# A two-layer attention and expert kernel with its engine loops written out, its waits on constants and its extra semaphore steps left out

## The chip, the cores and the metric

The kernel runs on one core of a Trainium2 chip, in one launch. The metric is the device time of that launch in microseconds, the median of several runs. The five engines of the core run streams of their own (TensorE or PE, VectorE or DVE, ScalarE or ACT, GpSimd or POOL, SyncE or SP), and meet only at semaphores. ScalarE, GpSimd and SyncE also issue DMA transfers from their streams.

## The reference

The input x is 16 batches of 512 tokens with 128 features in float32. Each of two layers adds an attention and an expert network to x, both taken of the same normalised rows:

```python
x = L0_attn_x
xn = _layernorm(x, axis=-1)
x = x + _L0_attn_ref(xn, ...) + _L0_ffn_ref(xn, ...)
xn = _layernorm(x, axis=-1)
x = x + _L1_attn_ref(xn, ...) + _L1_ffn_ref(xn, ...)
```

Layer 0 attention is causal, with 4 query and 2 key heads of 32 features, normalised queries and keys. Its expert network takes the 2 best of 16 experts of 256 hidden features (GELU). Layer 1 attention has 16 query and 4 key heads of 8 features, without a mask, a position factor on queries and keys, and the softmax's shift by the row maximum. Its expert network takes the best of 8 experts of 352 hidden features (SiLU, gated).

## The kernel before

The program is a row of blocks, and between blocks all engines meet: setup, layer 0 attention, a group table, the layer 0 experts, layer 1 attention, a second group table, the layer 1 experts.

**Attention, both layers.** The 16 batches are a software pipeline of which every engine writes its part as `body(i, o)` for batch 2i + o: the batch's own scores, exponentials and values, the end of the batch before (output projection and store), and the start of the next one to three (load, statistics, norms, projection, transposes). The helper `bodies` runs it: batches 0 to 2 and 13 to 15 are straight code, batches 3 to 12 are a hardware loop of five passes with two batches each, so each engine jumps back four times.

```python
def bodies(eng, body):
    for o in range(3):
        body(0, o)
    with eng.Fori(1, 6) as i:
        body(i, 1)
        body(i, 2)
    for o in range(13, NB):
        body(0, o)
```

In layer 0 a batch goes round a ring: VectorE's `square_sums` (L372) frees GpSimd's `factors` (L529 to L534); on GpSimd follow the scatter of the rows of the batch before to the experts' buffers (L544) and `norms` of the batch after (L512 to L518); VectorE normalises its rows (L357), PE transposes and projects them, ScalarE squares the projections, and VectorE sums them again. In layer 1 each batch has 64 score tiles on PE twice, once for the row maximum (L1834, reduced by VectorE at L1605, eight steps ahead) and once for the exponentials (L1806, ScalarE at L1511), and 16 steps of values (L1819). VectorE's stream also holds the router (`choose`, L1657, its first instructions once a batch, at step 0) and the statistics of the batch after next (L1696, step 2), which wait for GpSimd's `combine` (L1354 to L1358) of rows gathered by indirect DMA (L1343).

**Experts, both layers.** Tokens are packed in groups of 256 rows of one expert, 80 groups in layer 0 and 40 in layer 1, in a ring of 8 buffers. `pipeline` writes 8 groups as one turn of the ring: the first and the last turn are straight code, the eight (layer 0) or three (layer 1) between are a loop with `i` in a register. SyncE loads the rows of a group from an address in a table, ScalarE stores the results of the group before (L1087) and then issues the weights for the group eight ahead, also from the table (L1081, L1082), between its own activations (L1078). PE transposes the rows (L1035, copied by VectorE at L1112), multiplies by the first weights (L1047) and by the second (L1057).

**Waits.** With `i` in a register, a wait such as `wait_ge(x_used, b + 1)` needs its number computed in registers first. Where such a wait stands ahead of a DMA, an indirect DMA or another wait, the kernel puts a step of its own between them, an instruction that only counts up a semaphore that nobody reads. `passed` is that step, and `link_apart` is `link` (count up, wait for it on the same engine) with that step behind it:

```python
def passed(eng, count):
    eng.sem_inc(count, 1)
```

These steps are carried out in straight code as well, since the bodies are the same functions.

Of the kernel before, what the change touches and what calls it, by code (L numbers as in the profile page):

```python
# [10 lines left out]
ALU = mybir.AluOpType  # L11
# [5 lines left out]
NB, L = 16, 512  # L17
# [7 lines left out]
QKV0 = D + 2 * KV0 * DH0  # L25
# [15 lines left out]
NBUF = 8  # L41


class Chain:
# [25 lines left out]
def passed(eng, count):  # L70


    eng.sem_inc(count, 1)  # L73
# [143 lines left out]
def layer0_attention(nc, k, x_d, base_d, meta_d, xs_d):  # L217


    with ExitStack() as ctx:  # L220
# [72 lines left out]
        with nc.Block() as block:  # L293

            @block.sync
            def _(sp):
                def load(i, o):
                    b, h, p = batch(i, o)
                    sp.wait_ge(x_used, b + 1)
                    passed(sp, k.passed_sp)  # L300
                    sp.dma_start(x[:, p], x_d[bass.ds(b * L, L), :].rearrange("(t p) d -> p t d", p=P)).then_inc(x_in[p], 16)

                def store_meta(i, o):
                    b, h, p = batch(i, o)
                    sp.wait_ge(meta_ready, b + 1)
                    passed(sp, k.passed_sp)
                    sp.dma_start(meta_d[bass.ds(b * P, P), :], meta[:, p]).then_inc(meta_out[p], 16)

                def store_base(i, o):
                    b, h, p = batch(i, o)  # L310
                    sp.wait_ge(wo_used, b + 3)
                    passed(sp, k.passed_sp)
# [21 lines left out]
            def _(dve):  # L334
# [4 lines left out]
                def statistics(i, o):  # L339
# [6 lines left out]
                    ln.link_apart(last)  # L346
# [43 lines left out]
                def choose(i, o):  # L390

                    b, h, p = batch(i, o)
                    heads.link_apart(nc.vector.tensor_tensor(lg[:], prj[:, :, QKV0:PRJ0],
# [3 lines left out]
                    heads.link_apart(last)  # L397
# [100 lines left out]
            def _(pool):  # L498
# [3 lines left out]
                def norms(i, o):  # L502
# [8 lines left out]
                    passed(pool, k.passed_pool)  # L511
# [3 lines left out]
                    ln.link_apart(nc.gpsimd.tensor_tensor(tmp4[:, 2], tmp4[:, 1], mv[:, :, 1], ALU.mult))  # L515
# [5 lines left out]
                def factors(i, o):  # L521
# [7 lines left out]
                    fc.link_apart(nc.gpsimd.tensor_tensor(ftmp[:, 0], ss[:], bc, ALU.mult))  # L529
# [8 lines left out]
                def scatter(i, o, c):  # L538
                    b, h, p = batch(i, o)
                    if c == 0:  # L540
                        pool.wait_ge(meta_ready, b + 1)
                        passed(pool, k.passed_pool)
# [363 lines left out]
def expert_ffn(nc, k, layer, xs_d, ys_d, w_d, name, meta_d=None, base_d=None):  # L906
# [12 lines left out]
    with ExitStack() as ctx:  # L919
# [21 lines left out]
        with nc.Block() as block:  # L941

            @block.sync
            def _(sp):
# [13 lines left out]
                with sp.Fori(1, n_grp // NBUF) as i:  # L958
# [10 lines left out]
            def pipeline(eng, rows_of, up, down):  # L969
# [17 lines left out]
                with eng.Fori(1, last) as i:  # L987
# [9 lines left out]
            def _(pool):  # L997
                def put_rows(j, i, q):

                    pool.wait_ge(y_sb, j + 1)  # L1000
                    passed(pool, k.passed_pool)
# [157 lines left out]
def layer1_attention(nc, k, ys_d, base_d, meta_d, rf_d, rows2_d, qparts_d, kparts_d):  # L1159
# [6 lines left out]
    with ExitStack() as ctx:  # L1166
# [67 lines left out]
        with nc.Block() as block:  # L1234

            @block.sync
            def _(sp):
                def load(i, o):
                    b, h, p = batch(i, o)
                    if not (isinstance(b, int) and b < 2):  # L1240
                        sp.wait_ge(comb_done, b - 1)
                        passed(sp, k.passed_sp)
# [3 lines left out]
                def put_k(i, o):  # L1246
                    b, h, p = batch(i, o)
                    sp.wait_ge(kl_ready, b + 1)
                    passed(sp, k.passed_sp)
                    sp.dma_start(kparts_d[p].rearrange("j r l -> r j l"), kp[:]).then_inc(k_out[p], 16)  # L1250

                def put_q(i, o):
                    b, h, p = batch(i, o)
                    sp.wait_ge(ql_ready, b + 1)
                    passed(sp, k.passed_sp)
                    sp.dma_start(qparts_d[p].rearrange("j r l -> r j l"), qp[:]).then_inc(q_out[p], 16)

                def k_stack(i, o):

                    b, h, p = batch(i, o)  # L1260
                    if not (isinstance(b, int) and b < 2):
                        sp.wait_ge(s_ps, 64 * (b - 1))
                        passed(sp, k.passed_sp)
                        sp.wait_ge(mx_ps, 64 * (b - 1))
                        passed(sp, k.passed_sp)
                    sp.wait_ge(k_out[p], 16 * (h + 1))
                    passed(sp, k.passed_sp)
# [4 lines left out]
                def q_stack(i, o):  # L1272
# [3 lines left out]
                    passed(sp, k.passed_sp)  # L1276
# [16 lines left out]
                def shift(i, o, g):  # L1293
                    b, h, p = batch(i, o)
                    sp.wait_ge(sh_ready, 4 * b + g + 1)
                    passed(sp, k.passed_sp)
# [35 lines left out]
            def _(pool):  # L1332
                def gather(i, o, rows, s=None):
# [7 lines left out]
                    passed(pool, k.passed_pool)  # L1341
# [18 lines left out]
                def norms(ln, i, o):  # L1360
# [5 lines left out]
                    passed(pool, k.passed_pool)  # L1366
# [3 lines left out]
                    ln.link_apart(nc.gpsimd.tensor_tensor(tmp4[:, 2], tmp4[:, 1], mv[:, :, 1], ALU.mult))  # L1370
# [16 lines left out]
                def v_rows(i, o):  # L1387
# [4 lines left out]
                    passed(pool, k.passed_pool)  # L1392
# [3 lines left out]
                def k_parts(pc, i, o):  # L1396
# [4 lines left out]
                    pc.link_apart(nc.gpsimd.tensor_tensor(kr[:], k32[:], kp[:, 0, :], ALU.subtract))  # L1401
# [3 lines left out]
                def q_parts(pc, i, o):  # L1405
                    b, h, p = batch(i, o)
                    pool.wait_ge(qT_sb, b + 1)
                    pc.link_apart(nc.gpsimd.tensor_tensor(qr[:], q32[:], qp[:, 0, :], ALU.subtract))
# [4 lines left out]
                def normal_rows(i, o):  # L1413
# [5 lines left out]
                    passed(pool, k.passed_pool)  # L1419
# [5 lines left out]
                def keep_xn(i, o):  # L1425
# [4 lines left out]
                    passed(pool, k.passed_pool)  # L1430
                    nc.gpsimd.tensor_copy(row[:, p, :, 0:D], xn[:, p]).then_inc(kept_xn, 1)

                def scatter(i, o, t, s=None):
# [6 lines left out]
                    passed(pool, k.passed_pool)  # L1440
# [156 lines left out]
            def _(dve):  # L1597
# [52 lines left out]
                def choose(i, o):  # L1650
# [3 lines left out]
                    passed(dve, k.passed_dve)  # L1654
# [3 lines left out]
                    pro.link_apart(last)  # L1658
# [31 lines left out]
                def statistics(i, o):  # L1690
# [6 lines left out]
                    ln.link_apart(last)  # L1697
# [374 lines left out]
```

## Time and profile before

| | us |
|---|---|
| median of 3 runs | 1857.05 |
| lowest, highest run | 1851.42, 1863.5 |
| profiled execution | 1872.54 |
| its span, first to last instruction | 1870.8 |
| mean granted TensorE clock | 0.933 of full |
| PE, VectorE, ScalarE, GpSimd busy | 1590.7, 1231.6, 939.0, 831.1 |
| DMA transfers | 165.01 MB |

A program was profiled once, and all rows below are of that execution. Busy time is what each engine's instructions took; register, branch and semaphore instructions do not count as busy and are seen only as idle time of the engine ahead of its next instruction. That idle time is given in brackets behind a row with what ended it; "issue" means that no semaphore's update explains it. Line numbers are those of the kernel before. Layer 0 attention lies from about 70 to 485 us, its experts from 505 to 680 us, layer 1 attention from 685 to 1655 us, its experts from 1685 to 1860 us.

### The profile page before, as it was taken

How to read it: one execution, taken by the hardware profiler on the slowest of the kernel's cores; microseconds unless marked ns; L12 is line 12 of the kernel's file. 1: busy time of each engine (PE TensorE's matmuls, PEld its weight loads, DVE VectorE, ACT ScalarE, POOL GpSimd, SP SyncE). 2: the span in 40 equal slices, each digit the busy share in tenths (PEclk: the TensorE clock that was granted, in tenths of full speed). 3: DMA queues.
4: the chain of work that ended last, by engine and by line, in shares of the span. 5: the costliest groups of instructions: out<-in, count | busy, mean ns of one | idle time of the engine just before them, and what ended most of it. 6: DMA issues, size and time to landing. Idle time of an engine off the chain costs nothing. (4 is left out here: it accounts for less than half of the span.)

```text
span 1870.8 us, 35103 instructions
## 1 busy us (share of the span) xinstructions
PE 1590.7 (85%) x9488; PEld 825.8 (44%) x9488; DVE 1231.6 (66%) x3176; ACT 939.0 (50%) x1790; POOL 831.1 (44%) x987
## 2 busy tenths in 40 slices
PE   1688888888499954899999999999999999928997
PEld 0344444444298852233333333333333333308996
DVE  4466566657333335688888797888878899714443
ACT  1233433434143321577777676776767777712221
POOL 2465566556140024555555555455545541003444
PEclk9999999999799985699999899999999999969998
DMA  2011111111399951212112222122211111028772
GB/s 64 26 38 43 38 39 40 34 45 32 116 279 280 280 157 57 60 55 61 58 53 66 66 58 58 43 63 67 66 57 49 52 57 55 13 62 285 234 240 80
DMA packets 141468, 165.01 MB, mean 88 GB/s; under 512 B 28010, under 2 KB 114154, under 8 KB 140138
## 3 DMA queue, kind: packets, MB, share of 16 engines
q1 hardware_dynamic: 86628, 70.75, 13.1%
q10 hardware_dynamic: 40912, 62.62, 11.1%
q0 software_dynamic: 13824, 30.47, 5.3%
q8 instruction: 39, 0.64, 0.1%
q14 instruction: 65, 0.53, 0.1%
HBM read 111.93 MB, written 51.30 MB: 87 GB/s over the span
## 5 line engine op out<-in xcount | busy, mean ns | idle before, releaser
L1605 DVE TENSOR_REDUCE c_mx<-c_ps_mx 128x1 f32<-128x512 f32 x1024 | 650.4, 684 | 121.9 <-PE c_ps_mx L1834 99.3
L1511 ACT ACTIVATE c_pt<-c_ps_e 128x512 f32<-128x512 f32 x1024 | 557.7, 602 | 230.4 <-PE c_ps_e L1806 222.4
L1834 PE MATMUL c_ps_mx<-c_kex,c_qst 72*128 72x512 bf16 x1024 | 405.7, 399 | 34.1 <-DVE c_mx L1605 20.7
L1806 PE MATMUL c_ps_e<-c_qst,c_kex 74*128 74x512 bf16 x1024 | 396.1, 389 | 1.7 <-ACT c_pt L1511 1.0
L1819 PE MATMUL c_ps_v<-c_pt,c_vp 128*32 128x512 f32 x2048 | 280.6, 621 | 1.1 <-ACT c_pt L1511 0.7
L1834 PEld LDWEIGHTS c_ps_mx<-c_kex,c_qst 72*128 72x128 bf16 x1024 | 101.8, 99 | 355.4 <-DVE c_mx L1605 225.7
L1343 POOL DMA_INDIRECT c_gy<-ys,mt x128 | 124.0, 969 | 295.8 <-issue 161.8
L607 ACT ACTIVATE a_pt<-a_ps_s,temp 128x1024 f32<-128x1024 f32 (+3 forms) x128 | 112.7, 883 | 182.6 <-PE a_ps_s L698 110.4
L1047 PE MATMUL f_ps_h<-f_xT,f_w 128*128 128x256 f32 x800 | 195.5, 384 | 0.0
L695 PE MATMUL a_ps_s<-a_qT,a_kz 128*128 128x128 f32 (+3 forms) x512 | 181.7, 472 | 0.0
L544 POOL DMA_INDIRECT xs<-a_xn,a_meta x128 | 129.2, 1010 | 109.5 <-DVE a_meta L443 75.7
L1047 PEld LDWEIGHTS f_ps_h<-f_xT,f_w 128*128 128x128 f32 x800 | 144.7, 193 | 15.0
L1057 PE MATMUL f_ps_y<-f_w,f_h 128*128 128x128 f32 x1120 | 149.4, 280 | 1.0 <-ACT f_h L1078 0.2
L1057 PEld LDWEIGHTS f_ps_y<-f_w,f_h 128*128 128x128 f32 x1120 | 139.5, 192 | 19.3 <-ACT f_h L1078 12.9
L1441 POOL DMA_INDIRECT rows<-c_row,c_bsl x64 | 63.7, 996 | 158.2 <-PE c_ps_v L1819 127.1
L1806 PEld LDWEIGHTS c_ps_e<-c_qst,c_kex 74*128 74x128 bf16 x1024 | 101.3, 99 | 73.7 <-ACT c_pt L1511 15.0
L1003 POOL DMA_INDIRECT out<-f_y,f_x x80 | 76.6, 957 | 127.3 <-DVE f_y L1130 114.8
L1078 ACT ACTIVATE f_h<-f_ps_h,f_w 128x256 f32<-128x256 f32 x160 | 67.1, 470 | 97.3 <-PE f_ps_y L1057 63.6
L695 PEld LDWEIGHTS a_ps_s<-a_qT,a_kz 128*128 128x128 f32 x512 | 81.5, 198 | 60.9 <-issue 51.4
L1074 ACT ACTIVATE f_g<-f_ps_h 128x256 f32<-128x256 f32 x120 | 46.0, 383 | 118.1 <-PE f_ps_h L1047 98.9
L1134 DVE TENSOR_TENSOR f_y<-f_ps_y,f_w 128x256 f32<-128x256 f32 x80 | 34.0, 425 | 104.8 <-PE f_ps_y L1057 104.8
L1035 PE MATMUL f_ps_x<-ident,f_x 128*128 128x128 f32 x240 | 47.3, 280 | 59.7 <-DMA f_x<-rows 37.7
(231 smaller groups left out, 1990.9 us busy)
## 6 DMA issues: line engine op xcount, KB each, us to landing
f_w<-in_we ACTq DMA_DIRECT2D x80, 321.0 KB, 4.0
f_w<-in_we ACTq DMA_DIRECT2D x40, 576.0 KB
c_qst<-qparts SPq DMA_DIRECT2D x45, 384.0 KB
f_x<-rows SPq DMA_DIRECT2D x40, 257.0 KB
f_x<-xs SPq DMA_DIRECT2D x80, 128.0 KB, 3.9
ys<-f_y ACTq DMA_DIRECT2D x80, 128.0 KB, 3.6
qparts<-c_qp SPq DMA_DIRECT2D x16, 384.0 KB
c_kex<-kparts SPq DMA_DIRECT2D x48, 96.0 KB
```

What stands on the lines that cost most here:

```text
L544: nc.gpsimd.indirect_dma_start(xs_d, bass.IndirectOffsetOnAxis(ap=meta[:, p, c * NT + t:c * NT + t + 1], axis=0), xn[:, p, t, :], None).th ...
L607: nc.scalar.activation(pt[:, kt % 2, 2 * pr:2 * pr + 2, 0:n], ps_s[:, u % 2, :, 0:n], ACT.Exp, bias=k.temp[:, 3:4], scale=k.temp[:, 1:2]). ...
L695: nc.tensor.matmul(ps_s[:, u % 2, j, 0:L - kt * P], kz[:, p, head, kt * P:(kt + 1) * P], qT[:, p, kt * P:L], start=True, stop=False)
L1003: nc.gpsimd.indirect_dma_start(ys_d, bass.IndirectOffsetOnAxis(ap=x[:, q, t, 2 * D:ROW].bitcast(U32), axis=0), y[:, q, t, :], None).then_i ...
L1047: last = nc.tensor.matmul(ps_h[u][:, n, :], w[:, q, col:col + P], xT[:, q % 2, :], start=True, stop=True)
L1057: last = nc.tensor.matmul(ps_y[q % 2][:, t * D:(t + 1) * D], h[:, q % 2, c, t * P:(t + 1) * P], w[:, q, col:col + D], start=c == 0, stop=c ...
L1343: nc.gpsimd.indirect_dma_start(gy[:, p, n, :], None, ys_d, bass.IndirectOffsetOnAxis(ap=mt[:, p, n:n + 1], axis=0)).then_inc(gathered[p], 16)
L1511: nc.scalar.activation(pt[:, s % 4, hl, :], ps_e[:, ring_bank(p, n)], ACT.Exp, scale=QSCALE).then_inc(exp_done, 1)
L1605: nc.vector.tensor_reduce(mx[:, g % 2, n % 16:n % 16 + 1], ps_mx[:, ring_bank(p, n)], AX, ALU.max).then_inc(mx_done, 1)
L1806: nc.tensor.matmul(ps_e[:, ring_bank(p, n)], kex[:, p, hl, kt * P:(kt + 1) * P], qst[:, p, HL * g + hl, :], start=True, stop=True).then_in ...
L1819: last = nc.tensor.matmul(ps_v[32 * hl:32 * (hl + 1), :], vp[:, p, kt, hl, :], pt[:, s % 4, hl, :], start=kt == 0, stop=kt == NT - 1)
L1834: nc.tensor.matmul(ps_mx[:, ring_bank(p, n)], qst[0:SROW, p, HL * g + hl, qt * P:(qt + 1) * P], kex[0:SROW, p, hl, :], start=True, stop=Tr ...
```

## The change

All loops are written out: `bodies` is one Python loop over 16 batches, and `pipeline` and SyncE's loads loop in Python over the turns. So `i`, `j` and `b` are numbers everywhere, and every wait compares with a constant; where code asked whether a batch is an early one, it now finds the same number for all. `passed` and `link_apart` are gone: 21 calls of `passed` are dropped, and 10 linked steps become plain `link`. The work, its order on each engine, the buffers and the remaining semaphores are the same. The core of the diff:

```diff
 def bodies(eng, body):
-    for o in range(3):
-        body(0, o)
-    with eng.Fori(1, 6) as i:
-        body(i, 1)
-        body(i, 2)
-    for o in range(13, NB):
+    for o in range(NB):
         body(0, o)
...
-    def link_apart(self, ins):
-
-        self.n += 1
-        ins.then_inc(self.sem, 1)
-        self.eng.wait_ge(self.sem, self.base + self.n)
-        passed(self.eng, self.passed)
-
...
-                with sp.Fori(1, n_grp // NBUF) as i:
+                for i in range(1, n_grp // NBUF):
                     for q in range(NBUF):
                         load(NBUF * i + q, i, q)
...
-                with eng.Fori(1, last) as i:
+                for i in range(1, last):
                     for q in range(NBUF):
                         turn(i, q)
...
                     if not (isinstance(b, int) and b < 2):
                         pool.wait_ge(qkv_ready, b - 1)
-                    passed(pool, k.passed_pool)
                     ln.link(nc.gpsimd.tensor_scalar(tmp4[:, 0], mv[:, :, 1], EPS_LN, None, ALU.add))
...
-                    ln.link_apart(nc.gpsimd.tensor_tensor(tmp4[:, 2], tmp4[:, 1], mv[:, :, 1], ALU.mult))
+                    ln.link(nc.gpsimd.tensor_tensor(tmp4[:, 2], tmp4[:, 1], mv[:, :, 1], ALU.mult))
...
                     dve.wait_ge(prj_sb, NT * (b + 1))
-                    passed(dve, k.passed_dve)
...
                     sp.wait_ge(sh_ready, 4 * b + g + 1)
-                    passed(sp, k.passed_sp)
```

## Rows read from the trace of the kernel before

**Rows 1.** timeline of VectorE, layer 1's MAX8, one per batch: start us, us, engine, line

```profile
823.64 0.36 DVE L1657 MAX8 c_mx<-c_prj 128x8 f32<-128x8 f32 x4
...
931.73 0.36 DVE L1657 MAX8 c_mx<-c_prj 128x8 f32<-128x8 f32 x4
...
985.92 0.36 DVE L1657 MAX8 c_mx<-c_prj 128x8 f32<-128x8 f32 x4
...
1498.99 0.36 DVE L1657 MAX8 c_mx<-c_prj 128x8 f32<-128x8 f32 x4
...
1552.58 0.36 DVE L1657 MAX8 c_mx<-c_prj 128x8 f32<-128x8 f32 x4
```

**Rows 2.** windows around one jump back: length, busy us per engine, PEclk, DMA share, GB/s

```profile
1040.00:1045.00 5.00, 1.63 (x5) 0.49 (x5) 2.24 (x8) 1.61 (x4) 2.12 (x3) 0.89 0.39 115
1045.00:1050.00 5.00, 4.92 (x17) 1.69 (x18) 3.56 (x8) 1.75 (x3) 4.41 (x5) 0.50 0.01 2
```

**Rows 3.** timeline of VectorE after that jump

```profile
1042.54 1.29 DVE L1605 TENSOR_REDUCE c_mx<-c_ps_mx 128x1 f32<-128x512 f32 x2 [3.46 <-issue]
```

**Rows 4.** DMA queues, 1039 to 1046 us: packets, MB, share of 16 engines

```profile
q14 instruction: 3, 0.02, 0.8%
```

**Rows 5.** DMA queues, 550 to 670 us, all that it lists

```profile
q10 hardware_dynamic: 23515, 25.92, 76.6%
q1 hardware_dynamic: 16230, 7.52, 21.9%
```

**Rows 6.** DMA queues, 815 to 1030 us, the instruction queues

```profile
q8 instruction: 11, 0.18, 0.4%
q14 instruction: 13, 0.11, 0.2%
```

**Rows 7.** windows of layer 0 attention, batch by batch and eight in one

```profile
125.34:152.29 26.95, 22.69 (x145) 11.67 (x143) 17.12 (x59) 10.52 (x17) 16.20 (x19) 0.94 0.13 40
152.29:177.92 25.63, 21.47 (x145) 11.40 (x144) 17.23 (x59) 10.64 (x17) 15.99 (x19) 1.00 0.14 42
...
205.05:421.86 216.81, 182.29 (x1140) 94.30 (x1139) 137.34 (x466) 85.47 (x129) 128.74 (x152) 0.94 0.13 39
```

**Rows 8.** timeline of layer 0 attention, one batch, GpSimd and VectorE

```profile
259.53 0.22 POOL L529 TENSOR_TENSOR a_ftmp<-a_ss,a_r2sq 128x24 f32<-128x24 f32 x1 [3.35 <-DVE a_ss L372]
...
272.04 0.23 POOL L516 TENSOR_SCALAR a_tmp<-a_tmp 128x4 f32<-128x4 f32 x1 [0.19 <-POOL a_tmp L515]
272.35 1.04 POOL L517 TENSOR_TENSOR a_r<-a_tmp,mhalf 128x4 f32<-128x4 f32 x1
...
285.52 0.95 DVE L372 TENSOR_REDUCE a_ss<-a_sq 128x24 f32<-128x768 f32 x1 [7.28 <-ACT a_sq L586]
```

**Rows 9.** timeline of VectorE, layer 0 experts, one row per group of rows

```profile
518.74 0.41 DVE L1112 COPY f_xT<-f_ps_x 128x256 f32<-128x256 f32 x1
...
544.42 0.41 DVE L1112 COPY f_xT<-f_ps_x 128x256 f32<-128x256 f32 x1
...
662.56 0.41 DVE L1112 COPY f_xT<-f_ps_x 128x256 f32<-128x256 f32 x1
```

**Rows 10.** window of the layer 0 expert stage

```profile
530.00:550.00 20.00, 20.00 (x144) 18.87 (x144) 7.65 (x20) 7.81 (x19) 11.61 (x21) 1.00 0.98 306
```

**Rows 11.** waits, 550 to 665 us: us in total, times, longest

```profile
PEld f_ps_y L1057 <- ACT f_h L1078: 11.8, 42, 0.6
```

**Rows 12.** timeline of ScalarE's queue, straight turns of the layer 0 experts

```profile
526.54 0.75 ACTq L1082 DMA_DIRECT2D f_w<-in_we  x1
...
527.53 0.41 ACTq L1087 DMA_DIRECT2D ys<-f_y  x1
...
529.53 0.41 ACTq L1087 DMA_DIRECT2D ys<-f_y  x1
...
530.67 0.35 ACTq L1082 DMA_DIRECT2D f_w<-in_we  x1
```

**Rows 13.** timeline of VectorE in a late batch of layer 1

```profile
1226.26 0.87 DVE L1696 BATCH_NORM_STATS2 c_stats<-c_x 128x6 f32<-128x128 f32 x4 [1.36 <-POOL c_x L1358]
```

More of the change, by code:

```diff
@@ L345, in statistics @@
                         last = nc.vector.bn_stats(stats[:, t, :], x[:, p, t, :])
-                    ln.link_apart(last)
+                    ln.link(last)
                     for t in range(NT):
@@ L392, in choose @@
                     b, h, p = batch(i, o)
-                    heads.link_apart(nc.vector.tensor_tensor(lg[:], prj[:, :, QKV0:PRJ0],
+                    heads.link(nc.vector.tensor_tensor(lg[:], prj[:, :, QKV0:PRJ0],
                                                              k.br0[:].unsqueeze(1).to_broadcast([P, NT, E0]), ALU.add))
@@ L396, in choose @@
                         last = nc.vector.max(mx8[:, t, :], lg[:, t, :])
-                    heads.link_apart(last)
+                    heads.link(last)
                     for t in range(NT):
@@ L528, in factors @@
                     bc = r2sq[:].unsqueeze(2).to_broadcast([P, NT, H0 + KV0])
-                    fc.link_apart(nc.gpsimd.tensor_tensor(ftmp[:, 0], ss[:], bc, ALU.mult))
+                    fc.link(nc.gpsimd.tensor_tensor(ftmp[:, 0], ss[:], bc, ALU.mult))
                     fc.link(nc.gpsimd.tensor_scalar(ftmp[:, 1], ftmp[:, 0], 1e-24, None, ALU.max))
@@ L1000, in put_rows @@
                     pool.wait_ge(y_sb, j + 1)
-                    passed(pool, k.passed_pool)
                     for t in range(GT):
@@ L1295, in shift @@
                     sp.wait_ge(sh_ready, 4 * b + g + 1)
-                    passed(sp, k.passed_sp)
                     for n in range(2):
@@ L1369, in norms @@
                     ln.link(nc.gpsimd.tensor_tensor(tmp4[:, 1], rstd[:], rstd[:], ALU.mult))
-                    ln.link_apart(nc.gpsimd.tensor_tensor(tmp4[:, 2], tmp4[:, 1], mv[:, :, 1], ALU.mult))
+                    ln.link(nc.gpsimd.tensor_tensor(tmp4[:, 2], tmp4[:, 1], mv[:, :, 1], ALU.mult))
                     ln.link(nc.gpsimd.tensor_scalar(tmp4[:, 0], tmp4[:, 2], float(np.finfo(np.float32).eps), None, ALU.add))
@@ L1400, in k_parts @@
                     pool.wait_ge(kT_sb, b + 1)
-                    pc.link_apart(nc.gpsimd.tensor_tensor(kr[:], k32[:], kp[:, 0, :], ALU.subtract))
+                    pc.link(nc.gpsimd.tensor_tensor(kr[:], k32[:], kp[:, 0, :], ALU.subtract))
                     pc.link(nc.gpsimd.tensor_copy(kp[:, 1, :], kr[:]))
@@ L1407, in q_parts @@
                     pool.wait_ge(qT_sb, b + 1)
-                    pc.link_apart(nc.gpsimd.tensor_tensor(qr[:], q32[:], qp[:, 0, :], ALU.subtract))
+                    pc.link(nc.gpsimd.tensor_tensor(qr[:], q32[:], qp[:, 0, :], ALU.subtract))
                     pc.link(nc.gpsimd.tensor_copy(qp[:, 1, :], qr[:]))
@@ L1657, in choose @@
                         last = nc.vector.max(mx8[:, t, :], lg[:, t, :])
-                    pro.link_apart(last)
+                    pro.link(last)
                 def choose_index(i, o):
@@ L1696, in statistics @@
                         last = nc.vector.bn_stats(stats[:, t, :], x1[:, p, t, :])
-                    ln.link_apart(last)
+                    ln.link(last)
                 def moments(i, o):
```

18 lines of the change are left out of this document (removed).

## The prediction

> **What bounds the kernel now.** I read four views in this order: the page for the stages, the timeline of one instruction per batch for the pace of each stage, the timeline and windows around the places where the pace breaks, and the DMA view for code traffic. The profiled execution took 1872.54 us (span 1870.8 us), and the terms below are taken off that; the same saving then comes off the median of 1857.05 us, which lies 15.5 us lower. No engine bounds the whole. Each stage has its own limit, and the loops lie in the middle of all four stages, with the same batches written out before and after them. So the trace of before already shows the straight code beside the loop, and that comparison is my main tool.
>
> Layer 1 attention: the router's first MAX8 of a batch gives its pace [rows 1]. Batches 1 to 3 (straight) are 54.05 us apart on the mean (108.09 / 2, from 823.64 to 931.73), the last straight pair 53.59 (1498.99 to 1552.58). The first loop pair is 54.19 apart. From there the nine batches up to 1498.99 take 513.07 us, 57.01 each. Nine batches of a loop with two batches a pass and five passes hold its four jumps back.
>
> What a jump does is seen at 1040 us [rows 2, 3]: PE is busy 1.63 of 5 us, VectorE stands idle 3.46 us before its next row maximum with no semaphore behind it ("issue"), and in the next 5 us the granted clock is 0.50, that is 1.2 GHz instead of 2.4, after PE had idled. Code is what VectorE is waiting for: the DMA queue that carries instructions moves three packets in these 7 us [rows 4]. The layer 0 expert loop moves none in 120 us: the two data queues are all that its answer lists [rows 5]. The straight batches from 815 to 1030 us load 24 packets (11 and 13) [rows 6] and keep the 54 us pace, so code that is run in order is loaded ahead.
>
> Layer 0 attention is a ring of latencies: VectorE's sums of squares wait 7.28 us for ScalarE, GpSimd waits 3.35 us for them, and its factors, scatters and norms lead to the next rows [rows 8]. A straight batch takes 26.95 us with granted clock 0.94, a loop batch 27.10 (216.81 / 8) also at 0.94; one batch had no fall of the clock (1.00) and took 25.63 [rows 7].
>
> Layer 0 expert stage: the copy of the transposed rows comes every 1.98 us up to 544.42 (25.68 / 13), where the straight turns and the slack they left still carry it, and every 2.11 us after that (118.14 / 56) [rows 9]. In the loop PE waits for ScalarE's result, 42 times for 11.8 us [rows 11].
>
> **The change part by part.**
>
> Four jumps back and register waits, layer 1: thirteen batches lie between 823.64 and 1552.58, 728.94 us. At the straight pace, (108.09 + 53.59) / 3 = 53.89 us, they take 700.6. Gain 28.4 us: 9 x (57.01 - 54.19) = 25.4 for the jumps and what is late behind them, 10 x 0.30 = 3.0 for registers. Bounds: 25 (a late combine as in [rows 13] comes back here and there) and 31. After the jump PE also runs its first microseconds at half clock; that is inside the 25.4. The Trainium skill (page "Advanced Engine Details and Errata", section "Control Flow Timing") prices a compare-and-branch at about 108 ns. By that alone the four jumps would be worth 0.4 us as an estimate and the sum below about 22 us; the 3.46 us row speaks against using it, because that stall is not the branch but the code behind it.
>
> Registers, layer 0 attention: 27.10 - 26.95 = 0.15 us for ten batches, 1.5 us. No stall at the jumps shows in the 216.81 us, so nothing is taken for them.
>
> The extra semaphore steps: on GpSimd a linked step with one starts 0.19 us after its predecessor, one without 0.08 (272.04 + 0.23 to 272.35) [rows 8]. 0.11 x 2 (one in the factors, one in the norms; the norms' leading step runs ahead while GpSimd still scatters) = 0.22 us a batch on the ring, x 14 = 3.1 us. Layer 1 has three on VectorE a batch, whose price I take from the same two rows: 0.33 x 15 = 5 us if VectorE sets the pace alone, 0 if PE does; both are near full (PE and VectorE hand over at every row maximum), so I take 2. Those on SP come ahead of transfers with slots to spare, and cost nothing as long as a shift lands before its group; if that cover went, it would be 0.1 us a transfer. Stage starts, where everything is in one chain: some ten steps, 1 us.
>
> Clock falls of layer 0: a batch without one is 27.10 - 25.63 = 1.5 us shorter. The period shrinks by 0.37 us to about 26.7, which shifts PE's idle stretch against the falls. Bounds: 0 (each batch falls as now) and 18 us (none of twelve does). The straight batches here still fell, so I take two more spared, 3 us.
>
> Layer 0 expert stage: what holds ScalarE is its instruction stream, not its arithmetic. In straight code its DMA issues can follow each other at 1.14 us (529.53 to 530.67), 0.35 for the second, and 0.24 to the next turn's (526.54 + 0.75 to 527.53): 1.73 us a turn, below PE's 1.98 [rows 12]. In the loop each wait and each address is first computed, and around each jump it is worse. Without that PE's 1.98 is next: 118.1 - 56 x 1.975 = 7.5 us. The bound from below is 0: the transfers are at 98.5% of the engines' time [rows 5] at 279 GB/s, and need 299. Near 540 us they gave 306 over 20 us at share 0.98 [rows 10], so I take 7.5. The code of 64 turns must now be loaded as well, on the same engines: by the busy share of [rows 6] (0.6% for 215 us) below 1 us, taken as 0.5 lost.
>
> Layer 1 expert stage: no part of it shows a break; PE follows itself through it, so 0, and its code loads find transfers with room.
>
> Sum: 28.4 + 1.5 + 3.1 + 2 + 1 + 3 + 7.5 - 0.5 = 46.0 us. 1872.5 - 46 = 1826.5 for a profiled execution; 1857 - 46 = 1811 for the median.
>
> **The rivals.**
> (a) *Transfers bound the layer 0 expert stage.* For: 98.5% busy already. Against: 306 GB/s for 20 us. Price 7.5 us: 1818.5.
> (b) *Another wait takes the stall's place.* VectorE's statistics of batch b+2 sit in the same queue as the row maxima, and stand 1.36 us until GpSimd has combined the gathered rows [rows 13]. If the gather lands late in each of ten faster batches and costs about 1.8 us each time, 18 us are given back: 1829. Against: the straight batches show 53.6 to 54.05 with the same gather.
> (c) *The clock falls of layer 0 go altogether.* 12 x 1.5 = 18 instead of 3: 1796.
> (d) *Straight code starves its engines, slower than before.* The stretches that are loops now load almost no code [rows 5]; straight they need roughly 100 packets at the rate of [rows 6]. If such a load stops its engine for 3.46 us as in [rows 3], saving 46 is used up by 14 stops, and 19 more microseconds, so about 19 stops in all, make it slower by over 1%. If every second one stopped, 50 x 3.46 = 173 us: 1984. Against: 24 loads in [rows 6] without one stop. What speaks for it is only that none of these loads ran while the transfers were at 98% for long.
> (e) *The jumps cost what they cost for another reason,* something of every second batch, or the stall comes with the body's code and stays. Then only registers, steps and the expert stage remain: 46 - 25.4 = 20.6, 1836. Against: batches 1 to 3 are the same bodies without it.
>
> **How the numbers follow.** Chances: the forecast 0.55, (a) 0.13, (b) 0.11, (c) 0.13, (e) 0.04, (d) 0.02, and 0.02 for something not listed. The predicted time is 1811. The bounds of the unknown sizes around it (jumps 3, steps 3, falls 3, experts 7.5) give 1800 to 1824; taking in (c) below and (a) and (b) above makes 1795 to 1831, which leaves out (d), (e) and little else. A measurement of this kernel can tell about 1% from no change: 1838.5. Faster by over 1% is everything but (d), half of the unlisted, and a part of (e): 0.94; within 1%: 0.04; slower: 0.02.
>
> **What would show it.** In the profile after: no 3.46 us "issue" idle on VectorE and no window with granted clock 0.50 inside layer 1's steady batches; MAX8 of all batches 53.5 to 54.5 us apart; instruction packets evenly over all stages, some 100 to 150 more in all; layer 0 batches at 26.7 with a clock fall and 25.2 without; the expert copies every 1.98 us to the end; GpSimd's 0.19 us steps at 0.08. The prediction is wrong if single batches of layer 1 are still above 56 us with VectorE waiting for GpSimd's combine, if the expert copies are at 2.05 or more with PE waiting for a transfer, or if idle stretches marked "issue" show beside instruction packets.

## The result, and the profile after

The changed kernel takes 1792.74 us (median of 4 runs, 1789.77 to 1797.61), the kernel before beside it 1854.24 (4 runs, 1850.62 to 1863.5): ratio 0.9664, 95% interval 0.9618 to 0.9709, 61.5 us faster. The forecast was 1811, its range 1795 to 1831. The direction was right; the time lies 18.3 us below the forecast (15.5 of it are in the sum, 2.8 in the kernel before, which ran at 1854.24 instead of 1857.05) and 2.3 us below the range. One run of all those below, 1940.11 us of l1_dve_out at a granted clock of 0.821, was disturbed and does not count in that kernel's ratio.

The profiled execution after took 1790.67 us. The page of after, first line, granted clock in 40 slices, instruction queues, VectorE's costliest group:

```profile
span 1789.0 us, 29893 instructions
...
PEclk9999999999699965799999999999999999959998
...
q8 instruction: 78, 1.28, 0.3%
q14 instruction: 78, 0.64, 0.1%
...
L1567 DVE TENSOR_REDUCE c_mx<-c_ps_mx 128x1 f32<-128x512 f32 x1024 | 648.5, 682 | 89.5 <-PE c_ps_mx L1795 86.1
```

The 156 instruction packets lie in all stages. Before had 104 (39 and 65), so there are 52 more, not the 100 to 150 that the prediction expected: the loops of layer 1 had not been free of code traffic (27 packets from 1000 to 1500 us before, 45 after). VectorE's idle time before the row maxima is now nearly all a wait for PE (86.1 of 89.5 us); the "issue" of [rows 3] is gone. Timeline of VectorE after, the router's MAX8, one per batch (answers to [rows 1]):

```profile
833.70 0.36 DVE L1618 MAX8 c_mx<-c_prj 128x8 f32<-128x8 f32 x4
...
940.05 0.36 DVE L1618 MAX8 c_mx<-c_prj 128x8 f32<-128x8 f32 x4
...
993.17 0.36 DVE L1618 MAX8 c_mx<-c_prj 128x8 f32<-128x8 f32 x4
...
1472.11 0.36 DVE L1618 MAX8 c_mx<-c_prj 128x8 f32<-128x8 f32 x4
```

Twelve batches take 638.41 us from 833.70 to 1472.11, 53.20 each. No batch takes more than 53.51 us, and none is at the 53.9 that the prediction took for straight code. That is the first sign that more than the jumps went.

Windows after: two batches of layer 0, without and with a fall of the clock (answers to [rows 7]), and the layer 0 experts (to [rows 10]); columns: length, busy time of PE, PEld, DVE, ACT, POOL, then granted clock, DMA share, GB/s:

```profile
242.92:267.37 24.45, 21.13 (x144) 11.19 (x143) 17.23 (x59) 10.63 (x17) 16.17 (x19) 1.00 0.14 44
168.03:194.04 26.01, 22.70 (x144) 11.81 (x142) 17.21 (x59) 10.63 (x17) 16.17 (x19) 0.93 0.14 41
...
500.00:620.00 120.00, 120.00 (x852) 113.72 (x852) 46.12 (x122) 51.27 (x121) 9.41 (x18) 1.00 1.00 300
```

The batch with the fall is the only one in layer 0 (the prediction had 26.7 us with a fall and 25.2 without). The expert stage keeps PE busy all the time at 300 GB/s and a DMA share of 1.00: the forecast's limit and rival (a)'s limit are reached together. Its copies of transposed rows (answers to [rows 9]) come every 1.98 us to the end:

```profile
481.85 0.42 DVE L1088 COPY f_xT<-f_ps_x 128x256 f32<-128x256 f32 x1 [1.71 <-PE f_ps_x L1011]
...
634.89 0.41 DVE L1088 COPY f_xT<-f_ps_x 128x256 f32<-128x256 f32 x1
```

GpSimd in layer 0 after (answers to [rows 8]): the two linked steps that began 0.19 us behind their predecessor no longer have a gap that the view lists.

```profile
243.09 0.22 POOL L507 TENSOR_TENSOR a_ftmp<-a_ss,a_r2sq 128x24 f32<-128x24 f32 x1 [1.47 <-DVE a_ss L351]
243.40 0.28 POOL L508 TENSOR_SCALAR a_ftmp<-a_ftmp 128x24 f32<-128x24 f32 x1
...
255.10 0.20 POOL L493 TENSOR_TENSOR a_tmp<-a_tmp,a_mv 128x4 f32<-128x4 f32 x1
255.39 0.23 POOL L494 TENSOR_SCALAR a_tmp<-a_tmp 128x4 f32<-128x4 f32 x1
```

**The profiled execution before was no typical one.** It took 1872.54 us, while 1854 to 1857 is the median. So the same kernel was profiled once more:

> The kernel before, unchanged, looked at once more, because its profiled execution (1872.5 us) lay 18 us above its median while the changed kernel's (1790.7) lay on its median. Theory A: the profiled execution was as all others are, and is only stretched by something spread over it; then this one shows the same layer 0 batches (27.10 us with a clock fall in nearly each) and a time of 1850 to 1872. Theory B: the number of clock falls in layer 0 differs from execution to execution; then an execution near 1852 shows only two or three batches of 27.1 us and the others at 25.6 (eleven falls less by 1.5 us are 16 us), with layer 1 unchanged: four jumps back, 729 us for its thirteen batches.

It took 1852.16 us, span 1850.4. Theory B was right in kind, since the falls differ between two executions of one kernel, but not in its numbers. Two batches of layer 0 in that trace (windows, same columns):

```profile
122.92:147.80 24.88, 21.13 (x143) 11.10 (x142) 17.11 (x59) 10.53 (x17) 16.22 (x19) 1.00 0.14 43
147.80:174.15 26.35, 22.70 (x144) 11.73 (x143) 17.23 (x60) 10.75 (x17) 16.02 (x19) 0.94 0.13 42
```

The two kinds alternate: of thirteen batches seven have a fall of the clock, in the execution shown before it was eleven. Layer 0 attention, from its first reciprocal to its last output, took 391.1 us there and 375.7 here. The stages are therefore compared with this second trace. In it layer 1's pace breaks as in [rows 1 to 3]:

```profile
963.69 0.36 DVE L1657 MAX8 c_mx<-c_prj 128x8 f32<-128x8 f32 x4
1021.39 1.29 DVE L1605 TENSOR_REDUCE c_mx<-c_ps_mx 128x1 f32<-128x512 f32 x2 [3.48 <-issue]
1022.60 0.36 DVE L1657 MAX8 c_mx<-c_prj 128x8 f32<-128x8 f32 x4
```

Where the 61.4 us between the two spans went, from the timelines (us; layer 1: thirteen batches, MAX8 to MAX8):

| stage | before again | after | gain |
|---|---|---|---|
| layer 0 attention | 375.7 | 361.2 | 14.5 |
| layer 0 experts, first to last copy | 166.6 | 158.0 | 8.6 |
| layer 1 attention, 13 batches | 727.1 | 691.6 | 35.5 |
| all between and around them | 581.0 | 578.2 | 2.8 |

### The profile page after: what moved, and what is told of

It reads as the page before. It is cut to its first block and busy times, and to the rows that moved or that the text cites. A ratio compares the mean times of both kernels' runs of the same rounds, so it can differ in the third digit from the quotient of the medians.

```text
span 1789.0 us, 29893 instructions
## 1 busy us (share of the span) xinstructions
PE 1550.4 (87%) x9488; PEld 818.2 (46%) x9488; DVE 1227.7 (69%) x3176; ACT 937.3 (52%) x1789; POOL 831.6 (46%) x987
## 3 DMA queue, kind: packets, MB, share of 16 engines
q1 hardware_dynamic: 86628, 70.75, 13.7%
## 5 line engine op out<-in xcount | busy, mean ns | idle before, releaser
L1567 DVE TENSOR_REDUCE c_mx<-c_ps_mx 128x1 f32<-128x512 f32 x1024 | 648.5, 682 | 89.5 <-PE c_ps_mx L1795 86.1
L1795 PE MATMUL c_ps_mx<-c_kex,c_qst 72*128 72x512 bf16 x1024 | 400.1, 393 | 16.0 <-issue 8.0
L1767 PE MATMUL c_ps_e<-c_qst,c_kex 74*128 74x512 bf16 x1024 | 390.3, 383 | 1.7 <-ACT c_pt L1473 1.6
L1780 PE MATMUL c_ps_v<-c_pt,c_vp 128*32 128x512 f32 x2048 | 275.4, 610 | 1.1 <-ACT c_pt L1473 0.7
L1033 PEld LDWEIGHTS f_ps_y<-f_w,f_h 128*128 128x128 f32 x1120 | 143.5, 192 | 6.9 <-ACT f_h L1054 0.8
L1033 PE MATMUL f_ps_y<-f_w,f_h 128*128 128x128 f32 x1120 | 144.1, 275 | 0.4 <-ACT f_h L1054 0.4
```

The costliest lines, as they stand in the source:

```text
L1033: last = nc.tensor.matmul(ps_y[q % 2][:, t * D:(t + 1) * D], h[:, q % 2, c, t * P:(t + 1) * P], w[:, q, col:col + D], start=c == 0, stop=c ...
L1567: nc.vector.tensor_reduce(mx[:, g % 2, n % 16:n % 16 + 1], ps_mx[:, ring_bank(p, n)], AX, ALU.max).then_inc(mx_done, 1)
L1767: nc.tensor.matmul(ps_e[:, ring_bank(p, n)], kex[:, p, hl, kt * P:(kt + 1) * P], qst[:, p, HL * g + hl, :], start=True, stop=True).then_in ...
L1780: last = nc.tensor.matmul(ps_v[32 * hl:32 * (hl + 1), :], vp[:, p, kt, hl, :], pt[:, s % 4, hl, :], start=kt == 0, stop=kt == NT - 1)
L1795: nc.tensor.matmul(ps_mx[:, ring_bank(p, n)], qst[0:SROW, p, HL * g + hl, qt * P:(qt + 1) * P], kex[0:SROW, p, hl, :], start=True, stop=Tr ...
```

## The experiments

Theory A was the prediction's account; the question after the result was which part it had sized wrong. The stage times of all runs, read the same way as above:

| kernel | median us | layer 0 attention | batches with a fall | layer 0 experts | layer 1, 13 batches |
|---|---|---|---|---|---|
| before again | 1852.2 | 375.7 | 7 | 166.6 | 727.1 |
| steps_kept | 1822.1 | 375.4 | 7 | 158.1 | 703.7 |
| l1_dve_out | 1832.0 | 375.7 | 7 | 165.9 | 702.1 |
| l1_one_pass | 1827.6 | 375.1 | 7 | 166.6 | 703.5 |
| experts_act_out | 1848.6 | 373.9 | 6 | 157.7 | 727.6 |
| steps_dve | 1794.9 | 362.8 | 2 | 158.0 | 696.1 |
| steps_sp | 1792.1 | 366.1 | 4 | 158.0 | 691.8 |
| steps_pool | 1818.7 | 376.0 | 7 | 158.0 | 702.5 |
| steps_dma_only | 1805.5 | 362.8 | 2 | 158.1 | 700.5 |
| steps_not_dma | 1809.0 | 375.4 | 7 | 158.6 | 694.6 |
| scatter_early_1 | 1784.6 | 356.6 | 0 | 157.9 | 693.1 |
| scatter_early_2 | 1783.6 | 356.6 | 0 | 158.1 | 691.8 |
| after | 1792.7 | 361.2 | 1 | 158.0 | 691.6 |

The medians are of 4 runs (experts_act_out 10, before again 1); the other columns are of the one profiled execution, and the falls are those of the thirteen batches from the first reciprocal on. What the span holds beside these three stages is 574.9 to 585.7 us in the fourteen traces and does not follow the edits. Part of it is the start of layer 1: from the second to the third batch of the router it takes 62.5 us in one execution of the kernel before and 58.0 in the other.

**steps_kept: straight code and constant waits, steps left in.** The edit, against the changed kernel, wherever the change took a step out:

```diff
+                    passed(pool, k.passed_pool)
-                    ln.link(nc.gpsimd.tensor_tensor(tmp4[:, 2], ...))
+                    ln.link_apart(nc.gpsimd.tensor_tensor(tmp4[:, 2], ...))
```

> All loops written out as in the change, all extra semaphore steps kept. Theory A (the prediction's prices): the steps are worth 0.22 us a batch in layer 0 and 0.13 in layer 1, about 6 us in all, so this kernel stands at about 1799, layer 0 batches 24.7 us, layer 1 batches 53.4. Theory B: the straight batches of the kernel before (53.9 us in layer 1, 24.85 in layer 0 for batch 13) already show what the steps cost, 0.69 and 0.41 us a batch; then the layer 1 batches here are 53.9, layer 0 24.85, and the whole is 15 us over the changed kernel, 1808.

1822.12 us, ratio 0.9812 [0.9767, 0.9857]. So the steps cost 29 us of the 61.5 and the loops 32. The batches are those of theory B (24.88 us in layer 0, 54.13 in layer 1), but the whole is 14 us above it. The loops' part is layer 1 (23.4) and the layer 0 experts (8.5); layer 0 attention gains 0.3 us from straight code, within what its fall count moves. The steps' part is 12.1 in layer 1 and 14.2 in layer 0 (5.6 for a batch 0.43 us shorter, the rest for six falls that go with it). Another 5.5 us of the two traces' difference lie outside the three stages, where executions differ by as much.

**l1_dve_out: only VectorE's layer 1 loop written out, and l1_one_pass: all of layer 1 with registers kept, but no jump back.**

```diff
-                bodies(dve, body)
+                written_out(dve, body)
```
```diff
+def one_pass(eng, body):
+    for o in range(3):
+        body(0, o)
+    with eng.Fori(1, 2) as i:
+        for o in range(1, 11):
+            body(i, o)
+    for o in range(13, NB):
+        body(0, o)
```

> The kernel before with VectorE's loop of layer 1 attention alone written out; all other engines and stages keep loops and steps. Theory A (VectorE's code load is the stall at each jump): the 3.46 us idle goes at all four jumps, the batches after a jump fall from 57 to about 54.3 us, and the kernel gains about 23 us, to 1831. Theory B (every engine stalls at its own jump, or registers do): four other engines still jump at the same place, the batches stay above 56 us, gain under 6 us.

> The kernel before with the ten looped batches of layer 1 attention as one single pass of a loop on every engine: all register arithmetic, register waits and steps stay, no engine jumps back. Theory A (jumps are 25 us, registers 3): layer 1 batches 54.2 us throughout, 13 of them 704 us instead of 729, time 1829. Theory B (register waits are what is slow and pile up at the jumps): under 10 us gain.

1832.0 us, ratio 0.9872 [0.9815, 0.993], and 1827.63, ratio 0.9855 [0.9809, 0.9901]. Layer 1's thirteen batches fall to 702.1 and 703.5, as in steps_kept (703.7), and from 727.1. So one engine's jumps make all of the loss, as both theories A said, and computing waits in registers costs layer 1 nothing measurable. The prediction had set 3.0 us down for it.

**steps_dve, steps_pool, steps_sp: the changed kernel with the steps of one engine put back.** The edit is that of steps_kept, on one engine.

> The changed kernel with VectorE's extra semaphore steps put back (three a batch in layer 0, three in layer 1), none on GpSimd or SyncE. Layer 1 batches are 53.2 us without any step and 54.1 with all of them; layer 0 batches 24.44 and 24.88. Theory A (VectorE, which sets layer 1's pace, pays for its own three steps and no other step counts): 54.1 in layer 1, 0.3 us a step, 24.44 to 24.55 in layer 0. Theory B (0.11 us a step, as the prediction priced one on GpSimd): 53.5 in layer 1. Theory C (the steps on GpSimd or SyncE do it): 53.2.

> The changed kernel with GpSimd's extra steps put back alone. In layer 0 two of them lie on the ring: 0.22 us a batch by the prediction's price, 24.66; theory A says all of the 0.44 is GpSimd's (24.88), which would need twice that price or a third step. In layer 1, by theory A of the run before, 53.2 us a batch; by theory C 54.1: GpSimd's late combine or late rows would then hold VectorE's statistics or PE.

> The changed kernel with SyncE's extra steps put back alone. The prediction says nothing is lost as long as a shift lands before its group is scored: 53.2 us in layer 1, 24.44 in layer 0, the whole within 2 us of the changed kernel. The rival: the shift's transfers are late already and each of the four a batch passes its 0.1 us on, 53.6 us.

1794.94 (ratio 0.966 [0.9614, 0.9705]), 1818.72 (0.9797 [0.9752, 0.9842]) and 1792.06 (0.9642 [0.9597, 0.9688]). By these ratios neither VectorE's steps nor SyncE's can be told from the changed kernel (0.9664); those on GpSimd cost 26 us. VectorE was where the prediction had put layer 1's. The profiled execution of steps_dve was its slowest, 1802.64; what of its 696.1 us belongs to the steps is taken up below.

**Which of GpSimd's steps: steps_dma_only and steps_not_dma.** In the traces of the runs so far, gathers behind a step started late, so the step ahead of an indirect DMA was the new suspect.

```diff
 # steps_dma_only: in gather and in both scatter functions, and for the expert rows
+                    passed(pool, k.passed_pool)
                     for n in rows:
                         nc.gpsimd.indirect_dma_start(
```
```diff
 # steps_not_dma: ahead of norms, v_rows, normal_rows, keep_xn, and in the chains
+                    passed(pool, k.passed_pool)
                     ln.link(nc.gpsimd.tensor_scalar(tmp4[:, 0], ...))
```

> The changed kernel with only those steps of GpSimd's put back that stand in front of its indirect DMAs (gathers and scatters of layer 1, scatters of layer 0, output rows of layer 0's experts); the steps ahead of its arithmetic stay out. Theory A: the cost is in the indirect DMAs alone. In the traces so far a gather of layer 1 that waits for a matmul starts 0.306 us after that matmul's end when the wait is its own, and 0.819 us after it when a step stands ahead of it; with one such gap on the way to the combined x of each batch and one on layer 0's ring, this kernel is nearly as slow as the one with all of GpSimd's steps (1818.7): 1810 to 1820, a layer 1 batch of 53.9 to 54.1 us against 53.2, and VectorE's waits for the combined x come back (about 0.9 us a batch). Rival B: the steps ahead of the arithmetic cost it, some 0.07 us each on a row of them: this kernel stays at 1792 to 1798 and the next one is the slow one.

> The other half: all of GpSimd's steps back but those in front of indirect DMAs. Theory A: 1791 to 1800, a layer 1 batch of 53.2 to 53.4 us. Rival B: 1812 to 1820. If the two halves each give some 12 us, the cost is shared and both theories are half right.

1805.53 us, ratio 0.9729 [0.9698, 0.976], and 1808.99, ratio 0.9759 [0.9734, 0.9784]. By the whole times each half costs about as much (13 and 16 us), as the last sentence of the second expectation foresaw, and neither theory stands as written. By stages they are apart. The steps ahead of indirect DMAs cost layer 1 8.9 us and layer 0 1.6, which is one fall more at the same period (4.7 us more of that trace's difference lie outside the three stages). The steps in the arithmetic cost layer 1 3.0 us and layer 0 14.2.

*Layer 1.* The fifth gather of a batch waits for a step of values on PE. PE and GpSimd in the timelines, first steps_dma_only, then after:

```profile
938.20 1.06 PE L1798 MATMUL c_ps_v<-c_pt,c_vp 128*32 128x512 f32 x8
...
940.09 0.95 POOL L1327 DMA_INDIRECT c_gy<-ys,mt  x1 [1.07 <-PE c_ps_v L1798]
...
950.62 1.90 POOL L1338 TENSOR_TENSOR c_gy<-c_gy,mt 128x1024 f32<-128x1024 f32 x1 [2.82 <-DMA c_gy<-ys,mt]
...
955.25 0.87 DVE L1675 BATCH_NORM_STATS2 c_stats<-c_x 128x6 f32<-128x128 f32 x4 [0.85 <-POOL c_x L1342]
```
```profile
931.99 1.06 PE L1780 MATMUL c_ps_v<-c_pt,c_vp 128*32 128x512 f32 x8
...
933.36 0.96 POOL L1310 DMA_INDIRECT c_gy<-ys,mt  x1 [1.08 <-PE c_ps_v L1780]
...
943.57 1.90 POOL L1321 TENSOR_TENSOR c_gy<-c_gy,mt 128x1024 f32<-128x1024 f32 x1 [2.52 <-DMA c_gy<-ys,mt]
...
948.21 0.87 DVE L1657 BATCH_NORM_STATS2 c_stats<-c_x 128x6 f32<-128x128 f32 x4
```

The matmuls' group ends at 939.26 and the gather starts 0.83 us later; after, 933.05 and 0.31 us later. Of the 52 gathers of layer 1 in after before which GpSimd stood idle, 39 start 0.30 to 0.31 us behind the last matmul; in steps_dma_only these start 0.82 to 0.86 us behind it. The other 13, the first of each batch, have a waiting instruction ahead of them in both kernels, and differ little: 0.85 against 0.95. So a step that takes the wait makes the indirect DMA behind it start 0.51 us later than a wait of its own does. What follows the gather is in order on GpSimd: three parts of q, three more gathers, the combine, and VectorE's statistics. VectorE's waits over six batches, steps_dma_only, after, and steps_not_dma (us in total, times, longest):

```profile
DVE c_mx L1585 <- PE c_ps_mx L1813: 27.4, 60, 0.8
DVE c_stats L1675 <- POOL c_x L1342: 5.0, 6, 1.4
```
```profile
DVE c_mx L1567 <- PE c_ps_mx L1795: 27.4, 60, 0.8
DVE c_stats L1657 <- POOL c_x L1325: 0.6, 3, 0.3
```
```profile
DVE c_mx L1586 <- PE c_ps_mx L1814: 27.4, 60, 0.8
DVE c_stats L1676 <- POOL c_x L1340: 1.1, 5, 0.3
```

The wait for the combined x grows by 4.4 us in six batches, 0.73 each; the pace differs by 0.69 (8.9 / 13). All the rest of VectorE's waits is the same to the tenth. In this stage the statistics' wait ends last, and it begins at a gather.

The way from one batch's statistics to the next can be followed whole in these timelines. Means over the steady batches, us:

| leg of a layer 1 batch | after | steps_dma_only | steps_not_dma | steps_dve | steps_kept |
|---|---|---|---|---|---|
| VectorE's statistics to the end of the matmul that frees the fifth gather | 37.98 | 37.98 | 37.98 | 38.08 | 38.08 |
| end of that matmul to the gather | 0.31 | 0.82 | 0.30 | 0.30 | 0.82 |
| fifth gather to the last | 6.78 | 6.88 | 6.93 | 6.78 | 7.00 |
| last gather to the combine (its rows must land) | 3.50 | 3.57 | 3.59 | 3.73 | 3.60 |
| combine to the statistics | 4.64 | 4.63 | 4.63 | 4.65 | 4.63 |
| sum | 53.21 | 53.88 | 53.43 | 53.54 | 54.13 |

The sums agree with the pace of each kernel (thirteen batches in 691.6, 700.5, 694.6, 696.1 and 703.7 us). So the 0.93 us a batch between after and steps_kept are 0.51 at the gather, 0.22 on GpSimd from the fifth gather to the last (the parts of q and the gathers' own steps), 0.10 on VectorE and 0.10 in the landing of the rows. In steps_dve VectorE's steps make 0.10, or 1.3 us in thirteen batches. The other 3 us of its 4.5 are rows that landed later, mostly in its first three batches and the ninth; the landing varies from batch to batch in every trace (2.5 to 4.5 us), so differences of 1 to 3 us between two traces of layer 1 are not read as an effect of a step.

*Layer 0.* Timeline of GpSimd in steps_not_dma, which answers to the rows of after above:

```profile
250.74 0.22 POOL L522 TENSOR_TENSOR a_ftmp<-a_ss,a_r2sq 128x24 f32<-128x24 f32 x1 [1.45 <-DVE a_ss L365]
251.16 0.28 POOL L523 TENSOR_SCALAR a_ftmp<-a_ftmp 128x24 f32<-128x24 f32 x1 [0.20 <-POOL a_ftmp L522]
...
257.59 1.16 POOL L536 DMA_INDIRECT xs<-a_xn,a_meta  x1 [0.30 <-issue]
...
263.06 0.20 POOL L508 TENSOR_TENSOR a_tmp<-a_tmp,a_mv 128x4 f32<-128x4 f32 x1
263.46 0.23 POOL L509 TENSOR_SCALAR a_tmp<-a_tmp 128x4 f32<-128x4 f32 x1 [0.20 <-POOL a_tmp L508]
```

Each linked step costs 0.11 us (251.16 - 250.74 against 243.40 - 243.09; 263.46 - 263.06 against 255.39 - 255.10), as predicted. The second scatter takes 1.16 us where after has 0.96, in every batch of this trace: that is 0.20 more on the same ring. 0.11 + 0.11 + 0.20 = 0.42, and the batch without a fall is 24.87 us long against 24.44. Why the scatter is slower behind such steps stays open; in the traces with the loops kept and the steps in (before again, l1_dve_out) it is 1.16 and 0.96 us in turn, batch by batch.

**scatter_early_1 and scatter_early_2: a shorter ring.** One or two of a batch's second four scatters are moved into the 1.47 us in which GpSimd waits for VectorE's sums.

```diff
                     if nxt:
                         factors(i, o + 1)
-                    scatter(i, o, 1)
+                    scatter(i, o, 1, range(1, NT))
                     if nxt2:
                         norms(i, o + 2)
                     if nxt:
                         scatter(i, o + 1, 0)
+                        scatter(i, o + 1, 1, range(1))
```

> The changed kernel with one of the four second-half scatters of a layer 0 batch moved ahead of the factors of the next batch on GpSimd, into the 1.46 us in which it waits there for VectorE's sums. Theory: the ring GpSimd norms, VectorE normalise, meta and sums, GpSimd factors and scatters sets the 24.44 us of a layer 0 batch, and a scatter of 1.26 us is taken out of it: 23.2 us a batch, 13 to 16 us in all, 1776 to 1781, and no more clock falls than the changed kernel has. Rival: another ring (TensorE's projections, the transfers of the scattered rows) stands just behind: under 5 us, 1788 or more.

> Two of the four scatters moved. The second one no longer fits into the 1.46 us, so the factors start 1.1 us later while the norms start 2.5 us earlier. Theory of the ring: as the norms' earlier start counts whole and the factors' later one too, 22.9 to 23.2 us a batch, within 3 us of the kernel with one scatter moved. Rival: the factors' delay reaches TensorE, whose projections wait for them, and the batch is 24 us or more.

1784.57 us, ratio 0.9624 [0.9606, 0.9642], and 1783.61, ratio 0.9627 [0.9608, 0.9647]: both medians are below the changed kernel's, whose own interval (0.9618 to 0.9709) overlaps theirs. Layer 0 attention falls by 4.6 us, of which 1.6 is the one fall. The batch is 24.20 us in both, not 23.2 or 23.0, so another ring stood just behind, as the rivals said. Timeline of VectorE, first scatter_early_1, then after:

```profile
251.24 1.40 DVE L395 COPY a_kz<-a_ps_t 32x512 f32<-32x512 f32 x2
252.68 0.35 DVE L336 TENSOR_SCALAR a_xn<-a_x,a_mv,a_rstd 128x128 f32<-128x128 f32 x1
```
```profile
255.37 1.40 DVE L395 COPY a_kz<-a_ps_t 32x512 f32<-32x512 f32 x2
257.05 0.35 DVE L336 TENSOR_SCALAR a_xn<-a_x,a_mv,a_rstd 128x128 f32<-128x128 f32 x1 [0.28 <-POOL a_r2sq L496]
```

In after, the normalised rows wait 0.28 us for GpSimd; with the scatter moved they follow VectorE's own copies of k without a gap. Those copies wait 1.16 us for TensorE's transposes, and the sums of the next batch 5.18 us for ScalarE's squares of TensorE's projections, so the ring behind goes through VectorE, TensorE and ScalarE; the transfers that the rival also named do not show on it. The old ring was 0.24 us longer than this one (24.44 - 24.20), and the other 1.0 us bought nothing. Neither execution has a single clock fall in the thirteen batches of layer 0.

## Why the prediction was wrong, by its own steps

The sum was 46.0 us and the medians differ by 61.5. The terms, with what was measured:

| step of the prediction | predicted | measured | from |
|---|---|---|---|
| jumps and registers, layer 1 | 28.4 | 23.4 | before again, steps_kept |
| registers, layer 0 | 1.5 | 0.3 | the same |
| steps on layer 0's ring | 3.1 | 5.6 | 13 x 0.43, steps_kept and after |
| steps in layer 1 | 2 | 12.1 | 703.7 - 691.6 |
| stage starts, and the rest | 1 | 2.8 | last row of the stage table |
| clock falls, layer 0 | 3 | 8.6 | 14.5 - 5.6 - 0.3 |
| layer 0 experts, with the code loads | 7.0 | 8.6 | 166.6 - 158.0 |
| sum | 46.0 | 61.4 | spans |

**The step that failed** is "The extra semaphore steps", in its layer 1 part: 2 us on VectorE, at a bound of 5, where 12.1 were due, 10.9 of them on GpSimd (702.5 - 691.6). VectorE's own part, 1.3 us by its leg above, was near the 2; GpSimd's steps in layer 1 were put at nothing, without a reason. Two things went wrong in it. The price was taken from [rows 8], the gap of a linked step in front of an arithmetic instruction (0.11 us), and used for every kind; in front of an indirect DMA that waits it is 0.51 us, which no row shown gave. And the place was wrong: the prediction looked at VectorE and PE as the engines that are full and left out GpSimd, which is idle more than half of the time, although its own [rows 13] shows VectorE waiting 1.36 us for GpSimd's x. That wait was read as a rival that could take a gain back. It was the sign that everything ahead of x on GpSimd is on the path, and that making it shorter is a gain. The straight batches of before could not warn of it: they carry the steps as well, so the 53.89 us that were taken as the goal stand 0.69 above the 53.20 of after. With the steps and no loop all thirteen batches of steps_kept take 54.13, 0.93 above it (12.1 / 13).

**The clock falls** were the second largest error, with the direction right and the size wrong (3 against 8.6). Ordered by the batch length without a fall, the profiled executions have: at 24.87 us (before again, steps_kept, steps_pool, steps_not_dma, l1_dve_out, l1_one_pass) 7 batches of 13 with a fall, six times; at 24.74 (experts_act_out) 6; at 24.44 (after, steps_dve, steps_dma_only, steps_sp) 1, 2, 2 and 4; at 24.20 none, twice. So the number goes with the period, though not strictly: the first profiled execution of before had 11, and only 2 of its batches fell short of 26.9 us. In after the fall costs 26.01 - 24.44 = 1.57 us. The prediction lets a shorter period move the falls against PE's idle stretch and guesses that two go; the runs show six going for 0.43 us of period. No row of before showed what a shorter period does.

**Layer 1's jumps** were 5 us too dear: nine batches of 57.01 against 54.19 gave 25.4, and 3.0 were added for registers. l1_one_pass gives 23.6 for the jumps (727.1 - 703.5) and leaves nothing for registers. That it is VectorE's jump is shown by l1_dve_out: its stream alone written out recovers all of it. That it is the code behind the jump rests on the packets: two or three packets of the instruction queue q14 move during each of the four stalls of before, while the loop of layer 0, where no such packet moves from 205 to 425 us, has no stall; and with VectorE's stream written out q14 moves 12 packets from 1000 to 1500 us instead of 25. The four stalls of before again are 3.37 to 3.48 us, 13.7 together. The other 10 of the 23.6 follow them and were not measured apart; TensorE, idle in the stall, then runs at a granted clock of 0.50 for some 6 us (1022 to 1028 us). The Trainium skill (page "Runtime: NRT & Kernel Launch", section "Instruction fetch mechanics") says that code is prefetched strictly in sequence into a small buffer and that a block boundary is mostly hidden. This case agrees: in after 1.92 MB of code in 156 packets left no engine idle for over 1.2 us without a semaphore behind it between 780 and 1500 us, while a jump back, with instruction packets moving, cost it 3.36 to 3.48 us.

**The layer 0 experts** came out close to what was said (7.0 against 8.6), and by the engine that was named. experts_act_out writes out nothing but ScalarE's loop, in both expert stages:

```diff
+                if eng is straight:
+                    for i in range(1, last):
+                        for q in range(NBUF):
+                            turn(i, q)
```

> The kernel before with ScalarE's loop in both expert stages written out, the loops of all other engines and all of attention kept. Theory A (ScalarE's stream of register work, table loads and DMA issues holds the layer 0 experts at 2.11 us a group): the groups come every 1.98 us throughout as in the changed kernel, 166.6 us fall to 158, the whole by 8 us to about 1846. Theory B (PE's or SyncE's own jumps and registers do it): the pattern of 2.05 and 2.2 us stays, 166 us.

1848.55 us, ratio 0.9952 [0.993, 0.9974]; its stage takes 157.7 us, as after's 158.0. No run parts ScalarE's registers from its jumps in this stage. Rival (a) fell, if barely: the transfers gave the 300 GB/s that PE's pace needs, at a share of 1.00.

Of the rivals, (b), (d) and (e) are refuted by the even 53.2 us of all batches. (c) came true in good part: 7 falls to 1 in the typical execution, where its price had reckoned with twelve. Had layer 1's steps been sized at 12.1, the sum would have been 56 and the forecast 1801, 8 us off; with the falls at 8.6 as well it would have been 1795.

**The range** was too narrow for its own terms. Layer 1's steps had a bound of 5 and the falls one of 18, yet 3 stood for each in the range, and the four sizes that it names add up to 1802 and 1827.5, not to 1800 and 1824. Its lower end took (c) alone, where steps and falls missed on the same side. (One more slip: with the jumps at 0.4 us the sum would be 21.0, not about 22.)

What stays open: which step makes the second scatter of layer 0 slower by 0.20 us; how much of the 3.0 us that steps_not_dma adds to layer 1 is cost of the steps (0.15 us a batch between the gathers, 2 us in thirteen) and how much is the landing of the rows (the other 1); what makes the falls go with the period; and the 2.8 us around the stages, which differ from one execution to the next by as much.

## What to carry to other kernels

Read a wait such as "VectorE statistics, 1.36 us, released by GpSimd's x" as a path and walk it back through everything that stands in order ahead of x on its engine, idle as that engine may be; whatever shortens any of it is a gain, as long as the wait is there (in after 0.6 us in six batches are left of it). Price a small instruction by what stands behind it, not by its own length, and from a row of that kind. A comparison with straight code that lies in the same trace only shows what differs between the two, so a cost that both carry stays invisible. And before a sum is built on a profiled execution, see how far it is from the median and in which stage: here the falls of layer 0 made a stage 15 us longer than in the next execution.

## What the runs showed that was not expected

An indirect DMA of GpSimd with the wait on itself starts 0.31 us after the matmul's end; with a separate waiting step ahead of it, 0.82 us after. It repeats in 39 gathers of each trace (0.30 to 0.31 and 0.82 to 0.86).

Five engines jump back four times each in layer 1, and VectorE's stream alone accounts for the 24 to 25 us; the same loops on the four others cost nothing that the runs could tell.

The falls of TensorE's clock in layer 0 (granted clock 0.93 or 0.94 over a batch that has one, 1.00 over one that has none) go with a few tenths of a microsecond in the batch's length: 7 of 13 batches have one at 24.87 us, 1 to 4 at 24.44, none at 24.20. One more execution of the kernel before had 11, so the length is not all.
